# A gated FFN kernel with ternary weights: one x load, the weight sums and the first product of its opening stage rearranged

## The reference, cut to what matters

```python
# x: (128, 32, 256) = (batch, sequence, features); cond: (128, 128)
q  = relu(cond @ W3 + b3)                          # (128, 256)
x1 = (32 * x + x.sum(sequence)) * q[:, None, :]
c  = relu(x1 @ W2 + b2)                            # W2: (256, 256)
h1 = c @ ternary(w1).T ; h3 = c @ ternary(w3).T    # w1, w3: (682, 256)
out = x + (silu(h1) * h3) @ ternary(w2).T          # w2: (256, 682)
# ternary(w) = s * clip(round(w / s), -1, 1),  s = mean(|w|)
```

## Time and profile before

| what | value |
|---|---|
| median of 3 runs | 165.32 us (165.08 to 165.34) |
| the profiled execution's own time | 165.95 us |
| its span, first to last instruction | 164.2 us |
| PE busy | 159.7 us, 97% |
| DVE, ACT, POOL busy | 116.4, 89.6, 55.1 us |
| granted TensorE clock | 1.000 |

### The profile page before, as it was taken

One profiled execution on the slowest core, in us unless ns is written; L12 is line 12 of the kernel. 1 busy time (PEld: TensorE's weight loads), 2 busy tenths in 40 slices (PEclk: granted clock), 3 DMA queues, 4 the chain that ended last, 5 costly groups with the idle time before them and its releaser, 6 DMA issues.

```text
span 164.2 us, 2295 instructions
## 1 busy us (share of the span) xinstructions
PE 159.7 (97%) x764; PEld 131.1 (80%) x764; DVE 116.4 (71%) x187; ACT 89.6 (55%) x163; POOL 55.1 (34%) x53
## 2 busy tenths in 40 slices
PE   7999999999999999999999999999999999999992
PEld 4778787888887888788887888788887888788892
DVE  2566999978978891788548891888548870566863
ACT  4077888435844475345844466355744566255540
POOL 5014023402360276204841276204841266001500
PEclk9999999999999999999999999999999999999999
DMA  4997566665565589300250007000150006000063
GB/s 130 296 356 163 87 100 99 97 97 88 92 100 95 92 191 166 50 4 0 35 93 0 0 4 122 8 0 0 29 101 4 2 0 113 15 0 4 16 112 128
DMA packets 67412, 12.67 MB, mean 77 GB/s; under 512 B 63216, under 2 KB 67144, under 8 KB 67400
## 3 DMA queue, kind: packets, MB, share of 16 engines
q1 hardware_dynamic: 67248, 12.46, 38.7%
q10 hardware_dynamic: 152, 0.07, 0.1%
HBM read 8.32 MB, written 4.19 MB: 76 GB/s over the span
## 4 chain that ended last, share of the span: by engine, by line
PE 91%; DMA 4%; SPq 2%; issue 0%; DVE 0%
PE bank L538 49%; PE bank L581 21%; PE bank L469 15%; DMA xo<-in_x_dram 4%; PE bank L565 3%; PE bank L484 1%; PE bank L445 1%; SPq L212 1%; PE bank L496 0%; PE bank L478 0%; SPq L218 0%; SPq L217 0%; SPq L224 0%; SPq L216 0%; SPq L222 0%
## 5 line engine op out<-in xcount | busy, mean ns | idle before, releaser
L538 PE MATMUL bank<-c_hi,T 128*128 128x512 f32 (+1 forms) x176 | 69.2, 393 | 0.0
L538 PE MATMUL bank<-c_lo,T 128*128 128x512 f32 (+1 forms) x176 | 68.8, 391 | 0.0
L389 ACT ACTIVATE silu<-bank,checked 128x512 f32<-128x512 f32 (+1 forms) x48 | 33.1, 690 | 51.5 <-PE bank L538 51.3
L778 DVE SCALAR_TENSOR_TENSOR gf<-bank,out_scale,silu 128x512 f32<-128x512 f32 (+1 forms) x42 | 31.3, 744 | 34.7 <-PE bank L538 31.0
L538 PEld LDWEIGHTS bank<-c_hi,T 128*128 128x128 f32 (+1 forms) x176 | 32.8, 186 | 7.6 <-issue 0.2
L538 PEld LDWEIGHTS bank<-c_lo,T 128*128 128x128 f32 (+1 forms) x176 | 32.8, 186 | 7.3
L272 POOL TENSOR_TENSOR x<-y,qT 128x512 f32<-128x512 f32 x12 | 13.7, 1144 | 53.6 <-DVE y L685 53.6
L469 PE MATMUL bank<-x,W_sb 128*128 128x256 f32 x128 | 29.5, 381 | 0.4 <-DMA W_sb<-in_L_cond_W_dram 0.4
L581 PE MATMUL bank<-g_hi,T 128*128 128x512 f32 x70 | 28.5, 407 | 0.0
L786 DVE TENSOR_TENSOR g_lo<-gf,g_hi 128x512 fp32r<-128x512 f32 x40 | 28.5, 712 | 0.0
L581 PE MATMUL bank<-g_lo,T 128*128 128x512 f32 x70 | 27.3, 390 | 0.0
(11 more groups left out here) (78 smaller groups left out, 108.8 us busy)
## 6 DMA issues: line engine op xcount, KB each, us to landing
xb<-in_x_dram SPq DMA_DIRECT2D x64, 64.0 KB, 2.7
out_dram<-turned SPq DMA_DIRECT2D x28, 128.0 KB, 2.7
xo<-in_x_dram SPq DMA_DIRECT2D x3, 256.0 KB, 4.7
w_sb<-in_L_ffn_w_dram SPq DMA_DIRECT2D x2, 384.0 KB, 6.3
w_sb<-in_L_ffn_w_dram SPq DMA_DIRECT2D x1, 682.0 KB, 8.4
w_sb<-in_L_ffn_w_dram SPq DMA_DIRECT2D x2, 256.0 KB
xo<-in_x_dram SPq DMA_DIRECT2D x1, 512.0 KB, 4.9
xo<-in_x_dram SPq DMA_DIRECT2D x2, 128.0 KB, 2.5
```

The source lines that it names most:

```text
L389: nc.scalar.activation(silu[r, m % 2, :], h1[j % 2][r], ACT.Silu, scale=checked[r, 0:1]).then_inc(silu_done, 1)
L538: last = pe.matmul(dst[j % 2][0:w, :], T13[:, k, col:col + w], part[:, g % NC, k, :], start=(i == 0), stop=(i == len(passes) - 1))
L778: nc.vector.scalar_tensor_tensor(out=gf[r, m % 3, :], in0=second, scalar=out_scale[r], in1=silu[r, m % 2, :], op0=ALU.mult, op1=ALU.mult). ...
```

## The change

Five edits, all in the opening stage:

1. SP issues half 3 of x straight after half 2, ahead of the wait and of w1's DMAs.
2. `sum_partitions(0)` and `sum_partitions(1)` move into project_c(2) and project_c(3), between the products for the first and the second 128 output columns.
3. The scaling of half 0 is done in two instructions of 256 columns, one for each half of the input features, and its product runs over input features outside and output columns inside, so that its first two products need only the first instruction.
4. The filler's operands are a constant of ones that the launch itself writes, in place of `blank`; DVE's memset of it is gone.
5. Reordering: on DVE scale_mixed(3) goes ahead of limit(0) and above_limit(0) of w1's part 0; on PE the transposes of w3's part 0 go from behind project_c(3) to behind h1_step(0), and h1_step(1) follows them; h3_step(1) goes ahead of the transposes of w3's part 1 and of sum_partitions(2).

Order on PE after: ..., project_c(1), mix_x(3), project_c(2) with sum_partitions(0) inside, transpose w1 part 0, project_c(3) with sum_partitions(1) inside, h1_step(0), transpose w3 part 0, h1_step(1), h3_step(0), transpose w1 part 1, h3_step(1), transpose w3 part 1, sum_partitions(2), h1_step(2), h3_step(2), transpose_w2.

```diff
             load_half(2)
+            load_half(3)
 
             sp.wait_ge(zeroed, 2)
             load_w13(w1_sb, w1, got_w1)
-            load_half(3)
             load_w13(w3_sb, w3, got_w3)
...
+            def project_first():
+                z = z_of(0)
+                for k in range(DC):
+                    if k:
+                        pe.wait_ge(x1_done, 1)
+                    else:
+                        pe.wait_ge(first_part_done, 1)
+                    for c in range(DC):
+                        last = pe.matmul(z[:, c, :], W2_sb[:, k, c * P:(c + 1) * P], x1[:, 0, k, :],
+                                         start=(k == 0 and c == 0), stop=(k == DC - 1), skip_group_check=True)
+                last.then_inc(z_done, 1)
...
                 for c in range(DC):
+                    if c and n in (2, 3):
+                        if n == 2:
+                            pe.wait_ge(const_ready, 4)
+                        else:
+                            pe.wait_ge(q_ready, DC)
+                        sum_partitions(n - 2)
                     for k in range(DC):
...
-            pe.wait_ge(blank_ready, 1)
+            filler = nc.const_aps.tensor(1.0, [P, BANK], BF16)
             for _ in range(WARM_UP):
-                pe.matmul(bank[:, 7, :], blank[:], blank[:].unsqueeze(1).broadcast_to([P, BANK // P, P]), start=True, stop=True)
+                pe.matmul(bank[:, 7, :], filler[:, 0:P], filler, start=True, stop=True)
...
             pe.wait_ge(got_W2, 16)
-            project_c(0)
+            project_first()
             mix_x(2)
             project_c(1)
             mix_x(3)
-            pe.wait_ge(const_ready, 4)
-            sum_partitions(0)
             project_c(2)
 
             pe.wait_ge(x1_done, EARLY - 1)
             transpose_w13(0, 0, w1_t)
-
-            pe.wait_ge(q_ready, DC)
-            sum_partitions(1)
             project_c(3)
-            transpose_w13(1, 0, w3_t)
...
             h1_step(0)
+            transpose_w13(1, 0, w3_t)
+
+            h1_step(1)
             pe.wait_ge(relu_done, DC * HALVES)
             pe.wait_ge(T3_copied, 1)
             h3_step(0)
             transpose_w13(0, 1, w1_t)
 
-            h1_step(1)
+            h3_step(1)
             transpose_w13(1, 1, w3_t)
 
             pe.wait_ge(relu_done, DC * (EARLY - 1))
             sum_partitions(2)
-            h3_step(1)
...
+            def scale_first():
+                dve.wait_ge(mixed_done, 1)
+                for k, done in enumerate((first_part_done, x1_done)):
+                    nc.vector.tensor_tensor(by_batch(x1[:, 0, k]), by_batch(mixed_of(0)[:, k * HT:(k + 1) * HT]),
+                                            qT[:, 0, k].unsqueeze(2).broadcast_to([P, HB, S]), ALU.mult).then_inc(done, 1)
...
-            nc.vector.memset(blank[:], 0.0).then_inc(blank_ready, 1)
...
-            scale_mixed(0)
+            scale_first()
             scale_mixed(1)
             sum_sequence(SUMMED)
             add_sum(SUMMED)
             scale_mixed(SUMMED)
             early_lo(0)
+            scale_mixed(3)
             limit(0)
             above_limit(0, w1_sb, w1_t, parts[0])
-            scale_mixed(3)
             limit(1)
```

More of the change, by code:

```diff
@@ L99, in adaln_ternary_ffn_kernel @@
         mix = sb("mix", [P, P], F32)
-        blank = sb("blank", [P, P], BF16)
         warm = sb("warm", [P, 1], F32)
@@ L160, in adaln_ternary_ffn_kernel @@
         zeroed = sem("zeroed")
-        blank_ready, mix_ready = sem("blank_ready"), sem("mix_ready")
+        mix_ready = sem("mix_ready")
+        first_part_done = sem("first_part_done")
         condT_done, condT_copied = sem("condT_done"), sem("condT_copied")
@@ L508, in keep_busy @@
                 for _ in range(n):
-                    pe.matmul(bank[:, 7, 0:P], blank[:], blank[:], start=True, stop=True)
+                    pe.matmul(bank[:, 7, 0:P], filler[:, 0:P], filler[:, 0:P], start=True, stop=True)
             keep_busy(2)
```

## The result

| | us |
|---|---|
| before, median of 7 (165.08 to 166.18) | 165.82 |
| after, median of 7 (166.09 to 167.53) | 167.03 |
| ratio, 95% interval | 1.007 [1.0046, 1.0095] |
| after, the profiled execution (span 164.3) | 166.09 |

What follows compares the result with a forecast made beforehand. PE, busy 97% of the span, was taken to bound the kernel, then the chain of waits through half 3's DMA. Terms 0.05 - 0.10 + 0.24 gave +0.2 us: 165.32 to 165.5, range 164.9 to 166.2.

Steps and rivals of the forecast that it cites:

- the margin of 0.4 us: On DVE and POOL: POOL's rounding would have to end 0.4 earlier for its subtraction to start ahead of above_limit(0).
- the first product waits for W2 at 7.04: Opening of PE: the first product stays held by W2's load until 7.04, after 0.40 us of idle time.
- w1's landing at 11.29: Loads: w1's last DMA takes half 3's old place and lands at 11.29, making relu(1) on ACT 0.62 later.
- POOL gets in first: Slower rival: POOL's subtraction starts before above_limit(0), transposes of w1 1.0 later, +1.2 in all, 166.5; chance 0.13.
- The forecast's own sum: At transpose_w2: 0.05 later at w1's transposes, 0.10 back at the second sum, 0.24 lost, giving +0.2 us.
- Wait for w1's transposes: PE behind project_c(2): waits 0.45 for above_limit(0), so w1's transposes start at 14.32, 0.05 later than before.
- Second sum without a wait: sum_partitions(1) inside project_c(3): the wait for ACT's sums of w3 goes, 0.1 net saved (0 to 0.25).
- the 0.24 I took: New wait at transpose_w2 for above_limit(2), with sum_partitions(2) behind h3_step(1): late by 0.20 to 0.28.
- The total of +0.2 us: Whole kernel: profiled execution from 165.95 to 166.15, median from 165.32 to 165.5.
- The cover of the first sum: project_c(2): the old order had the whole product behind sum_partitions(0) to hide DVE's work; the new one halves it.
- Split scaling and filler at nothing: Opening stage: splitting half 0's scaling and changing the filler gain 0 (bounds 0 to -0.2), only widening the wait for W2.
- the cover that the forecast gave it: Ahead of the first product: two scalings of 256 columns instead of one of 512 end long before W2 lands.

Runs made afterwards that it cites:

- e1: The changed kernel once more, nothing altered, for a second trace and more times: median 166.67, ratio 1.0049.
- e4: The changed kernel with the filler of before (zeros that DVE writes): median 166.84, ratio 1.0061.
- e15: The kernel before with only scale_mixed(3) ahead of limit(0) and above_limit(0) on DVE, and w1's sum inside project_c(2): 166.98, ratio 1.0070.
- e16: The changed kernel with half 3 behind w1's loads again, POOL free: 167.12, ratio 1.0077.
- e2: The changed kernel with POOL's subtraction of half 1 also waiting for above_limit of w1's first part: 165.94, ratio 1.0019.
- e13: The changed kernel with w1's sum ahead of project_c(2) again, POOL free: 165.81, ratio 1.0005.
- e3: The changed kernel with DVE's limit of w1 also waiting for POOL's rounding of half 1, to put POOL first: 167.12, ratio 1.0086.
- e5: e2's kernel with w1's sum ahead of project_c(2) again: 166.21, ratio 1.0015.
- e7: e2's kernel with w1's sum ahead of project_c(2) and w2's sum ahead of h3_step(1): 165.80, ratio 0.9998.
- e6: e2's kernel with the transposes of w3's second part and the sum of w2 again ahead of h3_step(1): 165.80, ratio 1.0007.
- e10: e7's kernel without the five short fillers between the cond transpose and mix_x(1): 165.46, ratio 1.0011.
- e14: The changed kernel with scale_mixed(3) behind above_limit(0) again, POOL free: 166.53, ratio 1.0050.

## Why the prediction was wrong

**The step that failed** is the margin of 0.4 us by which DVE was to be ahead of POOL, above_limit(0) at 13.37 and POOL's subtraction at 13.75. Each was added up from a start that I took as fixed, and both moved against it.

The first is "the first product waits for W2 at 7.04", with the filler's part put at nothing. That held in the one trace of before. There W2 landed 4.3 us behind its issue; in the 17 other traces it took 3.3 to 3.9. In three traces of the changed kernel and its like with POOL free (the result, e1, e4) the product started at 7.21, 7.52 and 7.72, behind PE's own work at the slow rate. above_limit(0) hangs on it: it started at 13.44, 13.75 and 13.95, each 6.23 behind (the forecast had 13.37 - 7.04 = 6.33, so that part was right).

The second is w1's landing at 11.29. From it the forecast had POOL's rounding at 13.04; it was at 12.78, 12.84 and 12.98. And I had let POOL hang on the loads alone. ACT makes relu(0), w1's two sums and relu(1) in this order, and relu(0) waits for the first product. ACT in the result's trace, then in e4's:

```profile
9.21 0.84 ACT L331 ACTIVATE ct<-bank,b_cols 128x256 f32<-128x256 f32 x2 [5.47 <-PE bank L469]
...
11.90 0.82 ACT L331 ACTIVATE ct<-bank,b_cols 128x256 f32<-128x256 f32 x2
...
9.71 0.84 ACT L332 ACTIVATE ct<-bank,b_cols 128x256 f32<-128x256 f32 x2 [5.90 <-PE bank L470]
...
12.09 0.83 ACT L332 ACTIVATE ct<-bank,b_cols 128x256 f32<-128x256 f32 x2
```

In e4's, as in e15's and e16's, w1 is there in time and relu(1) follows relu(0) by 2.38. Then POOL's subtraction starts 6.06 to 6.14 behind the first product and above_limit 6.23 to 6.31: POOL is first by 0.16 or 0.17, with the product at 6.84 as with 7.72. DVE can be first only where w1 holds ACT back by more than that. In the result's trace relu(1) follows by 2.69, and DVE is first by 0.14; in e1's by 2.44, and POOL is first by 0.12. So the margin was no distance between PE and the loads: with the first sum inside project_c(2) and w1 in time it is on the wrong side.

The rival "POOL gets in first" had its mechanism, its place and nearly its price right (0.95 us at the transposes, where 1.0 was forecast). It named only an earlier w1 as the trigger, and its chance of 0.13 was far too low: 11 of 16 timed executions of the changed kernel lie at 166.6 or above, against 1 of the 12 of e2, in which POOL cannot be first. Only two of the 16 have a trace, one of each kind.

**Why the times form no groups.** The start of the first product runs from 6.43 (e13) to 7.79 (e3) over the 18 traces, and the changed kernel passes it on. From that start to the end of the timed execution it is 158.88 us in the result's trace and 158.89 in e2's, where DVE is first, and 159.81, 159.77, 159.79 and 159.75 in those of e1, e3, e4 and e16, where POOL is. So being second at the port costs 0.9 us, and the start adds a spread of over a microsecond to either case.

**The rule of the lock.** The Trainium skill, "SBUF — State Buffer", section "SBUF: two separate sides", calls the shared port pair an exclusive lock that the first holder keeps for its whole instruction. The runs agree in both directions: above_limit 1.58 to 1.71 us instead of 0.75 when POOL was first, POOL's subtraction 1.73 instead of 1.27 when DVE was.

**The forecast's own sum held, where POOL was second.** Wait for w1's transposes: forecast 14.32, measured 14.34 in the change's profile and 14.37 in e2's. Second sum without a wait: right. transpose_w2: forecast 24.0, measured 23.90; the wait there was smaller than the 0.24 I took. That w1's transposes came out right is in part luck: above_limit was to start at 13.37 and be held until 0.55 behind POOL's rounding, and ended at 14.19 because it started at 13.44, when the rounding (to 13.40) was over, and took its plain 0.75. The total of +0.2 us against +0.14 between the profiled executions, and against 1.0019 (+0.3 us; +0.13 between the medians) for e2. The cover of the first sum was indeed halved. That undoing it does not gain by the medians of e5 and e7 does not refute it: from the first product to the end the traces have 158.55 us in e5, 158.55 in e6 and 158.66 in e7, against 158.89 in e2. So one undoing alone is worth some 0.3 us there, both together (e7) only 0.2, and the varying start can hide that in medians of 12.

**Split scaling and filler at nothing:** e4 agrees for the filler. The split was not tried by itself; with the first product no longer behind W2 the cover that the forecast gave it is gone, so its price stays open.

**Open:** single executions of e5, e7 and e10 that took over 1.1 us more than all others of their kernel, which none of the traces shows; the median of e14.

## What to carry to other kernels

When an edit frees one engine's instruction earlier, ask which engine it now races for a port, and what each of the two hangs on, back to a start that they share. Here both hung on the first product, with POOL ahead, and only a late load kept it back; a margin that rests on a load against PE's start varies with both, and one profile cannot measure it. A profile that is the fastest of its set cannot explain a loss: take a second one. A single extra wait (here POOL's on `ternary_done`) settles such a race: it took the ratio from 1.007 to 1.0019. And where single executions differ by a variable start, compare traces from that start on.

## What the runs showed of the hardware

The moment at which PE's records go from the slow rate to the fast one, read here as TensorE's step from 1.2 to 2.4 GHz, differed from execution to execution by far more than I had thought. PE was busy from 0.8 or 1.0 us on in all traces, with the same work but for the filler's operand (e10 alone had fewer fillers). The four fp32 products of 128 columns by condT took 0.61 us in six traces, the first of before among them; in one they took 0.84, and in eleven 1.04 to 1.06, among them the second of before and both of the changed kernel. In e3's the four records behind them, from 5.64 on, took 1.20 instead of 0.71. The granted clock that the profile gives is 1.00 in the slow stretches as in the fast ones. In the kernel before, the first product started at 7.04, held by W2, in one trace, and at 7.51, behind PE's own slow work, in the other, and by the transposes of w1 only 0.05 us of it was left. The Trainium skill, "TensorE: Matmul & The Clock Gate", section "Part 1: The HAM clock gate", says that this moment differs between runs of one kernel, and gives 0.5 us to either side. The traces agree that it differs, but it is behind 5.6 us in e3's and ahead of 4.2 in that of before, a wider spread than the page's.
